# Dispatch of two experts ahead of the expert units, and of the other six inside the first units

## The reference, cut to what matters

```python
G, S, C = 8, 128, 40            # 8 groups of 128 tokens, 40 slots of each expert in a group
probs = softmax(t @ w_router)   # 8 experts
gate, idx = top_k(probs, 2)
prio = cumsum(mask) * mask - 1  # number of the token's slot at its expert
dispatch = one_hot(prio_se, C)                       # g s e c
combine = dispatch * gate_se[..., None]
expert_in = einsum('gsec,gsd->egcd', dispatch, xg)   # the dispatch
h = relu(einsum('egcd,edf->egcf', expert_in, wi))    # F = 1536
expert_out = einsum('egcf,efd->egcd', h, wo)
out = einsum('gsec,egcd->gsd', combine, expert_out)
```

## Time and profile before

| | us |
|---|---|
| median of 3 runs (lowest, highest) | 634.12 (633.56, 634.17) |
| the profiled execution | 634.23 |
| its span | 632.0 |
| PE busy, share of the span | 597.5, 95% |
| PE weight load busy | 504.7, 80% |
| VectorE busy | 397.8, 63% |
| ScalarE busy | 301.5, 48% |
| mean granted clock of TensorE | 0.986 |

### The profile page before, as it was taken

One profiled execution on the slowest core, in us unless ns is written; L12 is line 12 of the kernel. 1 busy time (PEld: TensorE's weight loads), 2 busy tenths in 40 slices (PEclk: granted clock), 3 DMA queues, 4 the chain that ended last, 5 costly groups with the idle time before them and its releaser, 6 DMA issues.

```text
span 632.0 us, 11972 instructions
## 1 busy us (share of the span) xinstructions
PE 597.5 (95%) x4473; PEld 504.7 (80%) x4473; DVE 397.8 (63%) x664; ACT 301.5 (48%) x419; POOL 172.3 (27%) x106
## 2 busy tenths in 40 slices
PE   1998999999999999999858999999999999999996
PEld 1886876666666666666857999999999999999994
DVE  6657666667676666632779886547654675457535
ACT  3554434445454545454455534445544455364523
POOL 0400055667776666679200000000000000000000
PEclk9999999999999999999968999999999999999999
DMA  8045054432234444102050534444254444442302
GB/s 264 6 84 127 2 124 85 83 71 60 59 63 83 83 83 83 39 2 101 4 184 2 185 117 149 150 142 159 77 153 148 149 149 131 146 154 93 113 1 100
DMA packets 37411, 63.33 MB, mean 100 GB/s; under 512 B 3865, under 2 KB 32895, under 8 KB 37247
## 3 DMA queue, kind: packets, MB, share of 16 engines
q1 hardware_dynamic: 37374, 62.83, 35.4%
HBM read 44.16 MB, written 1.57 MB: 72 GB/s over the span
## 4 chain that ended last, share of the span: by engine, by line
PE 86%; DVE 6%; ACT 2%; POOL 2%; DMA 1%; issue 1%; SPq 1%; POOLq 0%; DVEq 0%
PE ps L758 20%; PE ps L774 20%; PE ps L551 13%; PE ps L560 9%; PE ps L537 7%; PE ps L461 7%; POOL acc L395 2%; DVE rhalf L1124 2%; PE ps L729 2%; PE ps L491 1%; PE ps L784 1%; DMA onehot<-c_onehot 1%; PE ps L584 1%; PE ps L791 1%; PE ps L792 1%
## 5 line engine op out<-in xcount | busy, mean ns | idle before, releaser
L1124 DVE TENSOR_REDUCE rhalf<-ps 128x1 f32<-128x512 f32 x192 | 131.4, 690 | 45.1 <-PE ps L537 44.0
L917 ACT ACTIVATE prob<-ps 128x1024 f32<-128x1024 f32 x96 | 98.0, 1026 | 101.4 <-PE ps L551 90.2
L395 POOL TENSOR_TENSOR acc<-acc,prob 128x1024 f32<-128x1024 f32 x48 | 115.6, 2407 | 4.6
L551 PE MATMUL ps<-qst,kst 128*128 128x512 f32 x384 | 110.9, 394 | 0.0
L758 PE MATMUL ps<-xeh,wih 128*128 128x320 f32 (+1 forms) x288 | 89.7, 312 | 1.0 <-ACT xeh L979 1.0
L774 PE MATMUL ps<-hh,woh 128*128 128x320 f32 x288 | 89.3, 310 | 0.0
L774 PE MATMUL ps<-hl,woh 128*128 128x320 f32 x288 | 89.0, 309 | 0.0
L758 PE MATMUL ps<-xel,wih 128*128 128x320 f32 (+1 forms) x288 | 89.0, 309 | 0.0
L758 PE MATMUL ps<-xeh,wil 128*128 128x320 f32 (+1 forms) x288 | 89.0, 309 | 0.0
L774 PE MATMUL ps<-hh,wol 128*128 128x320 f32 x288 | 89.0, 309 | 0.0
L551 PEld LDWEIGHTS ps<-qst,kst 128*128 128x128 f32 x384 | 71.8, 188 | 15.3 <-issue 0.8
(11 more groups left out here) (157 smaller groups left out, 908.4 us busy)
## 6 DMA issues: line engine op xcount, KB each, us to landing
raw_i<-in_L_ffn_wi SPq DMA_DIRECT2D x32, 576.0 KB, 4.9
raw_o<-in_L_ffn_wo SPq DMA_DIRECT2D x32, 576.0 KB, 4.0
xs<-in_x SPq DMA_DIRECT2D x8, 384.0 KB, 4.7
qst<-qh SPq DMA_DIRECT2D x12, 256.0 KB, 3.2
qst<-relh SPq DMA_DIRECT2D x12, 256.0 KB, 3.9
qst<-relw SPq DMA_DIRECT2D x12, 256.0 KB, 4.5
kst<-kp SPq DMA_DIRECT2D x12, 256.0 KB, 5.1
qst<-ql SPq DMA_DIRECT2D x12, 128.0 KB, 3.2
```

The source lines that it names most:

```text
L395: nc.gpsimd.tensor_tensor(acc[:, :], acc[:, :], prob[:, t % SLOT, :], ALU.add).then_inc(sum_add, 1)
L551: last = mm(bank(2 * (t % 2) + half), kst[b][:, part, t * P:(t + 1) * P], qst[b][:, part, half * BANK:(half + 1) * BANK], start=part == 0, ...
L917: run(prob[:, t % SLOT, :], ps[:, 2 * (t % 2) * BANK:2 * (t % 2 + 1) * BANK], ACT.Exp).then_inc(exp_done, 1)
L1124: ve.tensor_reduce(rhalf[:, p // 2, p % 2:p % 2 + 1], bank(4 + p % 2), AX_X, ALU.max).then_inc(max_red, 1)
```

## The change

The slot table is made in five parts. The first instruction covers experts 0 and 1 of all eight groups (640 values again); four others cover experts 2 to 7 of two groups each (480 values). Ahead of the units TensorE dispatches experts 0 and 1 alone: 6 steps, each 4 matmuls of 80 columns for the high and 4 for the low part, one bank for each part and four steps deep. The other six experts are dispatched by 12 late steps, each 2 matmuls of 240 columns for each part, all in banks 6 and 7, placed by `between` behind blocks 0, 2, 3 and 5 of iterations 0 to 2; ScalarE and VectorE copy them (480 values) in their iterations 1 to 3. `dg` goes from iteration 0 to iteration 3 on VectorE, and `slot_side` from iterations 1 to 3 to iterations 4 to 6 of TensorE and from 2 to 4 to 5 to 7 of VectorE. `pos` gets a place in SBUF of its own, since it is now read for longer.

```diff
+        FIRST_E = 2
+        EARLY, LATE = 2 * DC, DC * NT // XT
+        LATE_AT = [0, 2, 3, 5]
...
-            STEPS = DC * NT // XT
-            for n in range(STEPS):
-                b, c, first_g = dispatched(n)
-                pe.wait_ge(dsp_ready, n // DC + 1)
+            pe.wait_ge(dsp_ready, 1)
+            for n in range(EARLY):
+                c, half = n % DC, n // DC
                 for part, (x_, left) in enumerate(((th, xe_act), (tl, xe_dve))):
-                    wait(pe, left, n - 1)
-                    for g in range(first_g, first_g + XT):
-                        last = mm(bank(b + 2 * part + g - first_g, E * C), x_[:, g, c * P:(c + 1) * P],
-                                  dsp[:, g, :, :].rearrange("p e c -> p (e c)"), start=True, stop=True)
+                    wait(pe, left, n - 3)
+                    for g in range(HALF):
+                        last = mm(bank(2 * (n % 4) + part)[:, g * FIRST_E * C:(g + 1) * FIRST_E * C],
+                                  x_[:, half * HALF + g, c * P:(c + 1) * P],
+                                  dsp[:, half * HALF + g, 0:FIRST_E, :].rearrange("p e c -> p (e c)"), start=True, stop=True)
                     last.then_inc(xe_mm, 1)
+            def dispatch_late(n):
+                c, g = n % DC, n // DC * XT
+                pe.wait_ge(dsp_ready, n // DC + 2)
+                W = (E - FIRST_E) * C
+                for part, (x_, left) in enumerate(((th, xe_act), (tl, xe_dve))):
+                    pe.wait_ge(left, EARLY + n)
+                    for i in range(XT):
+                        last = mm(bank(6 + part)[:, i * W:(i + 1) * W], x_[:, g + i, c * P:(c + 1) * P],
+                                  dsp[:, g + i, FIRST_E:E, :].rearrange("p e c -> p (e c)"), start=True, stop=True)
+                    last.then_inc(xe_mm, 1)
...
                     def between(j):
-                        if k in (1, 2, 3) and j % 2 == 1:
...
+                        if first and k < UF and j in LATE_AT:
+                            dispatch_late(len(LATE_AT) * k + LATE_AT.index(j))
+                        if first and k in (4, 5, 6) and j % 2 == 1 and UF * (k - 4) + j // 2 < NT:
+                            slot_side(UF * (k - 4) + j // 2)
...
                     relu_low(k % 2, v, 0)
+                    late(0)
                     relu_low(k % 2, v, 1)
                     step(0)
                     relu_low(k % 2, v, 2)
+                    late(1)
+                    if first and k == 0:
+                        for i in range(1, NT // XT):
+                            slots_late(i)
                     if not (last and k + 2 >= PU):
                         split_wi(k % 2, v + 2)
                     step(1)
+                    late(2)
                     step(2)
                     if not (last and k + 1 >= PU):
                         split_wo((k + 1) % 2, v + 1)
-                    if first and k == 0:
+                    late(3)
+                    if first and k == UF:
                         dg
...
+            slots_late(0)
             split_wi(1, 1)
             split_wo(0, 0)
             pair(0, first=True)
```

More of the change, by code:

```diff
@@ L66, in metaformer_layer @@
     dpc = place("dpc", [PS, NT, P], F32R, w0)
+    pos = place("pos", [P, NT, E], F32, w0 + 4 * NT * P)
+    assert 4 * NT * P + 4 * NT * E <= 4 * DC * D
     ident = new("ident", [P, P])
@@ L153, in metaformer_layer @@
     end, at[0] = at[0], at[0] - 8 * UF * D
-    lg, ex, pr, mk1, mk2, cm1, cm2, pos = (
-        new(n, [P, NT, E]) for n in ("lg", "ex", "pr", "mk1", "mk2", "cm1", "cm2", "pos"))
+    lg, ex, pr, mk1, mk2, cm1, cm2 = (
+        new(n, [P, NT, E]) for n in ("lg", "ex", "pr", "mk1", "mk2", "cm1", "cm2"))
     top8 = new("top8", [P, NT, 8])
@@ L242, in metaformer_layer, with early_input, late_input @@
         TURN_BANKS, SUM_BANKS, AHEAD = [6, 0, 1, 2], [7, 3, 4, 5], 3
[L244 to L254, removed]
+        FIRST_E = 2
+        EARLY, LATE = 2 * DC, DC * NT // XT
+        LATE_AT = [0, 2, 3, 5]
+        def early_input(n, part):
+            c, half = n % DC, n // DC
+            src = bank(2 * (n % 4) + part, HALF * FIRST_E * C)
+            return ((xeh, xel)[part][:, c, 0:FIRST_E, half * HALF * C:(half + 1) * HALF * C].rearrange("p e (g s) -> p g e s", g=HALF),
+                    src.rearrange("p (g e s) -> p g e s", g=HALF, e=FIRST_E))
+        def late_input(n, part):
+            c, g = n % DC, n // DC * XT
+            src = bank(6 + part, XT * (E - FIRST_E) * C)
+            return ((xeh, xel)[part][:, c, FIRST_E:E, g * C:(g + XT) * C].rearrange("p e (g s) -> p g e s", g=XT),
+                    src.rearrange("p (g e s) -> p g e s", g=XT, e=E - FIRST_E))
         def weights(i):
@@ L721, in _ @@
             pe.wait_ge(tl_ready, NT)
-            STEPS = DC * NT // XT
-            for n in range(STEPS):
-                b, c, first_g = dispatched(n)
-                pe.wait_ge(dsp_ready, n // DC + 1)
+            pe.wait_ge(dsp_ready, 1)
+            for n in range(EARLY):
+                c, half = n % DC, n // DC
                 for part, (x_, left) in enumerate(((th, xe_act), (tl, xe_dve))):
-                    wait(pe, left, n - 1)
-                    for g in range(first_g, first_g + XT):
-                        last = mm(bank(b + 2 * part + g - first_g, E * C), x_[:, g, c * P:(c + 1) * P],
-                                  dsp[:, g, :, :].rearrange("p e c -> p (e c)"), start=True, stop=True)
-                    last.then_inc(xe_mm, 1)
-            pe.wait_ge(xe_act, STEPS)
-            pe.wait_ge(xe_dve, STEPS)
+                    wait(pe, left, n - 3)
[3 more added lines that the diff above has]
+                                  dsp[:, half * HALF + g, 0:FIRST_E, :].rearrange("p e c -> p (e c)"), start=True, stop=True)
+                    last.then_inc(xe_mm, 1)
+            pe.wait_ge(xe_act, EARLY)
+            pe.wait_ge(xe_dve, EARLY)
+            def dispatch_late(n):
+                c, g = n % DC, n // DC * XT
+                pe.wait_ge(dsp_ready, n // DC + 2)
[6 more added lines that the diff above has]
+                    last.then_inc(xe_mm, 1)
             def slot_side(n):
@@ L739, in slot_side @@
                     pe.wait_ge(dg_ready, 1)
+                    pe.wait_ge(xe_act, EARLY + LATE)
                 wait(pe, gsl_ready, n - 1)
@@ L814, in between @@
                     def between(j):
-                        if k in (1, 2, 3) and j % 2 == 1:
[L817 to L821, removed]
+                        if first and k < UF and j in LATE_AT:
+                            dispatch_late(len(LATE_AT) * k + LATE_AT.index(j))
+                        if first and k in (4, 5, 6) and j % 2 == 1 and UF * (k - 4) + j // 2 < NT:
+                            slot_side(UF * (k - 4) + j // 2)
+                        if not first and k in (1, 2, 3) and j % 2 == 1:
+                            combine_between(pr - 1, UF * (k - 1) + j // 2)
                     if not (last and k == PU - 1):
@@ L976, in _, with late_high @@
             split_wo(0, 0, 0)
-            for n in range(DC * NT // XT):
+            for n in range(EARLY):
                 act.wait_ge(xe_mm, 2 * n + 1)
-                run(*expert_input(n, 0), ACT.Copy).then_inc(xe_act, 1)
+                run(*early_input(n, 0), ACT.Copy).then_inc(xe_act, 1)
+            def late_high(n):
+                act.wait_ge(xe_mm, 2 * (EARLY + n) + 1)
+                run(*late_input(n, 0), ACT.Copy).then_inc(xe_act, 1)
             def relu(b, v, k):
@@ L1010, in step, with late @@
                         gated(pr - 1, n)
+                    def late(j):
+                        if first and 1 <= k <= UF:
+                            late_high(len(LATE_AT) * (k - 1) + j)
                     wait(act, y_mm, v - 1)
                     relu(k % 2, v, 0)
+                    late(0)
                     relu(k % 2, v, 1)
@@ L1264, in _, with slots_late, late_low @@
             step(ve.tensor_tensor(pos[:, :, :], cm1[:, :, :], cm2[:, :, :], ALU.add))
[L1265 to L1269, removed]
-                dve.wait_ge(xe_mm, 2 * n + 2)
-                ve.tensor_copy(*expert_input(n, 1)).then_inc(xe_dve, 1)
+            ge = [P, NT, FIRST_E, C]
+            ve.tensor_tensor(dsp[:, :, 0:FIRST_E, :], slot1[:, :].unsqueeze(1).unsqueeze(1).broadcast_to(ge),
+                             over(pos[:, :, 0:FIRST_E], C), ALU.is_equal).then_inc(dsp_ready, 1)
+            for n in range(EARLY):
+                dve.wait_ge(xe_mm, 2 * n + 2)
+                ve.tensor_copy(*early_input(n, 1)).then_inc(xe_dve, 1)
+            def slots_late(i):
+                ge = [P, XT, E - FIRST_E, C]
+                ve.tensor_tensor(dsp[:, XT * i:XT * (i + 1), FIRST_E:E, :], slot1[:, :].unsqueeze(1).unsqueeze(1).broadcast_to(ge),
+                                 over(pos[:, XT * i:XT * (i + 1), FIRST_E:E], C), ALU.is_equal).then_inc(dsp_ready, 1)
+            def late_low(n):
```

(11 more changed lines are left out.)

## The result

The changed kernel takes 646.53 us (644.60 to 647.43, 4 runs) where the kernel before takes 634.14 beside it: 1.0192 times as long, with an interval of 1.0166 to 1.0217, or 12.4 us. The forecast was 641.2 with a range to 646.5; the median lies on the upper edge of that range, 0.03 us above it. The profiled execution is the shortest of the four, 644.60 with a span of 642.8, 10.8 us more than the span before. But the dispatch begins 1.4 us sooner in it (332.76 against 334.18), though no instruction ahead of it was changed: 0.6 us of that stands already in attention (296.38 against 297.02 at the first matmul of the same line), and the rest comes about between there and the end of the router, whose matmuls met the high clock at other moments.

A forecast was written before the change was run, and what follows sets the result against it. TensorE was taken to bound the first pair of units, with slack only in the dispatch ahead; early start -3.5, late dispatch +5.8, first wait +1.9 and iteration boundaries +2.9 gave +7.1, 641.2 us, range 636.5 to 646.5.

The forecast's parts named there:

- late work: Late dispatch, 48 matmuls of 240 columns inside a stretch where TensorE is full: 0.12 us each, +5.8 us (bounds 5.4 and 7.1).
- The first wait: At late step 1 TensorE waits 1.9 us for bank 7, until VectorE has copied late step 0.
- each passage: From iteration 0 to 1 and 1 to 2, copies behind the splits of wo hold TensorE 1.45 us; 2.9 together.
- The slot side's free move: dg and the slot side's reads go where VectorE is busy 20.03 of 39.60 us, so they cost nothing.
- the load sets the early pace: Early 80-column matmuls are paced by weight loads: 0.21 us each at low clock, 0.111 at full; units start 3.5 us earlier.
- B: Rival: the load is hidden, early steps run at the column pace, units start 7.3 us earlier; 637.2 us, chance 0.12.
- C: Rival: early steps at the column pace and VectorE keeps up, so without its waits 632.2 us; chance 0.05.
- D: Rival: narrow matmuls stream slower, 240 columns costing up to 0.41 us; +18, 652 us, chance 0.05.
- from 334.18 to 337.85 at 0.21 are 17.5 matmuls; 30.5 more at 0.111 are 3.4 us: Early dispatch: the clock rises at 337.85, the last matmul starts at about 341.2, and the units start at 342.05.
- Rival A: The clock stays low in the early steps: units 3.2 us later, 1.5 lost in the first; 645.9 us, chance 0.18.
- the main case: The summed forecast, chance 0.60; its own range from 639.5 (waits 1.5 shorter) to 644 (upper bounds of the paces).
- The ceiling: Dispatch ahead of the units: hiding it could gain at most about 4.3 us, if dividing it cost nothing.

The follow-up runs named there:

- Experiment 4: Changed kernel with the fourth late copy of an iteration put ahead of the split of wo on ScalarE and VectorE: 642.92 us, 1.0128 against the kernel before.
- experiment 6: Changed kernel with 240-column early matmuls, fourth late copy ahead of the split of wo, late slot instructions 1 to 3 in VectorE's iterations 1 and 2: 638.16 us.
- experiment 5: Kernel before with only the slot side and dg moved to later iterations: 634.64 us, 1.0005 against the kernel before.
- experiment 1: Changed kernel with early matmuls writing 240 columns, the 80 repeated three times, same loads, copies and waits: 642.71 us, 1.0123 against the kernel before.
- experiment 3: Changed kernel with twenty idle 384-column matmuls, whose bank nobody reads, ahead of the dispatch: 642.34 us, 1.0133 against the kernel before.
- Experiment 7: Changed kernel with 240-column early matmuls, fourth late copy before wo's split, late slot instructions moved later, and twenty idle matmuls ahead of the dispatch: 635.00 us, 1.0001.

## Why the prediction was right or wrong

**Right: that it gets slower, and the sum of its lasting terms.** TensorE was the bound in the first pair, so late work costs its own length: 5.4 us, where I took 5.8 (0.1125 us a matmul, between my 0.111 by load and 0.1135 by columns, and not 0.12). The first wait was 1.8 us for 1.9 forecast (TensorE and VectorE both came to it 2.2 us later than counted, with the slow hidden 0), each passage 1.46 for 1.45, at late steps 1, 4 and 8 as named. Experiment 4 shows that the order made the passages; experiment 6 moves the late slot instructions away and the first wait falls by 1.05 us. The slot side's free move is confirmed by experiment 5.

**Right: the load sets the early pace.** 0.213 us a matmul, 0.21 forecast from the router's rows, and experiment 1 has the same 0.213 at 240 columns. Rivals B, C and D, which rested on another pace, are out: no early matmul ran at the column pace, and a matmul of 240 columns took 0.1125 us, less than one of 320 (0.147). The Trainium skill (TensorE: Matmul & The Clock Gate, Weight-path perf modes) says that weights of 128 columns load faster when they are not fp32; nothing of it is seen with the rounded type here, the pace at full clock being 0.111 to 0.113 us as for the router's fp32.

**Wrong: the clock.** The step that failed is "from 334.18 to 337.85 at 0.21 are 17.5 matmuls; 30.5 more at 0.111 are 3.4 us". I let the clock rise when it had risen under 320-column matmuls. It stayed low over all 48, so the units came after 11.06 us and not 7.87: 3.2 us. It then rose only 4.9 us into hidden 0, another 2.2. These 5.4 us and the 0.3 behind the waits, less the 0.4 on the late steps and 0.1 on the first wait, are the difference between +7.1 and +12.3. Rival A described this with 0.18 and 645.9 us (+11.8); it had the 3.2 exactly and 1.5 for hidden 0. The stated range held only because part of rival A lay inside it; the main case's own range, 639.5 to 644, missed. (Its upper end is written with +9.4 beside it; the upper paces give -1.9 + 7.1 + 1.9 + 2.9 = +10.0, which is the 644.) A's chance was too low: the profile had one stretch that pointed each way, the router's and the transposes', and I gave the transposes more weight because of their equally close loads, though they also have 128 columns where the router's have 8. Experiments 1, 3 and 7 settle that it is the early stream itself: wider alone lifts it in time, a clock that is up falls under 80 columns, and behind the same idle matmuls it stays up under 240. 10.2 us of back-to-back matmuls of 80 columns left the clock at 0.50 in the changed kernel's trace, and in experiment 3 they lost it. The Trainium skill's account (TensorE: Matmul & The Clock Gate, Part 1: The HAM clock gate) is that matmul activity releases the full clock, by time and not by the number of matmuls; these two traces do not agree with it.

**The ceiling.** I took "about 4.3 us" as the most that hiding could win. Experiment 7 won 5.1 us at the start, for its copies are of 320 values and no longer set the pace, and paid 6.9 back. The division doubles the number of weight loads, and a matmul of 80 or 240 columns takes 0.111 to 0.113 us where the undivided one of 320 takes 0.147: 96 matmuls at 0.1125 are 10.8 us of TensorE, 48 at 0.147 are 7.0.

**Still open.** The other three timed runs of the changed kernel took 646.1 to 647.4 us at a mean clock of 0.971 to 0.973, the profiled one 644.6 at 0.976. That fits a clock which rises later or sooner in these stretches, but those executions have no trace, so it is only argued.

## What to carry to other kernels

Work moved under a full engine is not hidden but added, and a step whose moving side is split in two pays its weight loads twice: compare the columns' time with the load's (0.11 us here) first. If matmuls become shorter than their loads, look at the granted clock as well, for a busy TensorE can run at half speed and hand that on to the work behind it. Where a copy frees a bank that an engine needs in the next step, it belongs ahead of everything in its queue that waits for that same engine's later work.

## What the runs showed of the hardware that I had not expected

TensorE's clock fell from 1.00 to 0.50 in the middle of an uninterrupted stream (experiment 3, 335.9 us, PE and its loads busy all of the time), and did not come back for 10.2 us, until 346.1, although 320-column matmuls ran from 340.8 on. So "busy" in the profile, of matmuls and of loads alike, did not tell here which clock would be granted.

The narrow stream's price goes on behind it: besides 0.1 us for each of its own 48 matmuls (0.213 against 0.111), it cost the first 18 matmuls of the units 0.12 us each (0.267 against 0.147), 2.2 us in all.
